# Relation layer of a four-layer graph network: two edge tiles in one expansion product, and keys loaded for two groups at once

## The reference, cut to what matters

```python
rel_in = jnp.concatenate([node_features[src], node_features[tgt]], axis=1)
for r in range(R):                                # R = 4 edge types
    mask = edge_type == r
    rel_t = _lrelu(rel_in @ W_R[r] + b_R[r])      # per edge
    Q = rel_t @ W_Q[r] + b_Q[r]; K = rel_t @ W_K[r] + b_K[r]; V = rel_t @ W_V[r] + b_V[r]
    e = _lrelu(jnp.concatenate([Q, K], axis=1) @ a_w + a_b)[:, 0]
    # softmax of e over the edges of one target and type, then
    h = h + jax.ops.segment_sum(V * attn[:, None], tgt, num_segments=num_nodes)
```

## Time and profile before

| What | Value |
|---|---|
| Time, median of 3 runs | 3078.84 us (3070.05 to 3078.93) |
| Span of the profiled execution | 3100.3 us |
| Own time of the profiled execution | not given apart; its span is 21.5 us over the median |
| PE, PEld busy in the whole span | 2081.7, 1679.2 us |
| DVE, ACT, POOL busy in the whole span | 1578.6, 1176.2, 1685.1 us |
| Group loop of the relation layer | from 107.5 us (first gather) to 800.9 us (last join) |

### The profile page before, as it was taken

How to read it: one execution, slowest core, us unless ns; L and a number is a source line. 1 busy time by engine, 2 the same in 40 slices (tenths; PEclk the granted TensorE clock), 3 DMA queues, 4 the chain that set the end, 5 groups by cost and what they waited for, 6 DMA issues and landing times. The chain is left out here.

```text
span 3100.3 us, 39481 instructions
## 1 busy us (share of the span) xinstructions
PE 2081.7 (67%) x9935; PEld 1679.2 (54%) x9935; DVE 1578.6 (51%) x4421; ACT 1176.2 (38%) x3344; POOL 1685.1 (54%) x1704
## 2 busy tenths in 40 slices
PE   5436777777765778788782356767777656555367
PEld 2235666666654667667671355556655433333267
DVE  4246767676751242423232434657688654444356
ACT  1245556555332223233231344445454322222244
POOL 3366656565104565565643666666646666666600
PEclk9655565656567889889986555555567665565589
DMA  6644444444103223232322444444432222222264
GB/s 223 233 139 128 129 114 136 117 126 115 41 19 86 71 67 80 65 80 65 81 64 73 126 119 120 115 125 123 124 98 70 75 69 78 71 71 72 65 242 141
DMA packets 244614, 322.44 MB, mean 104 GB/s; under 512 B 105346, under 2 KB 160931, under 8 KB 243045
## 3 DMA queue, kind: packets, MB, share of 16 engines
q0 software_dynamic: 66560, 163.90, 18.6%
q1 hardware_dynamic: 177797, 155.67, 16.6%
HBM read 257.60 MB, written 63.38 MB: 104 GB/s over the span
## 5 line engine op out<-in xcount | busy, mean ns | idle before, releaser
L1422 POOL DMA_INDIRECT e_gathered<-msg_src_table,src_idx x416 | 396.6, 953 | 420.9 <-issue 269.2
L703 POOL DMA_INDIRECT e_gathered<-rel_src_table,rel_idx x416 | 433.5, 1042 | 300.3 <-issue 245.6
L1971 POOL DMA_INDIRECT e_kv<-kv_table,src_idx x416 | 410.1, 986 | 275.3 <-issue 195.1
L1985 POOL DMA_INDIRECT rows_by_src<-e_kv,e_row x416 | 419.3, 1008 | 230.2 <-issue 202.0
L2059 PE MATMUL e_ps_q<-e_window,e_spread 64*128 64x128 f32 x1664 | 350.9, 378 | 151.8 <-ACT e_spread L2198 63.6
L2059 PEld LDWEIGHTS e_ps_q<-e_window,e_spread 64*128 64x128 f32 x1664 | 306.9, 275 | 223.8 <-issue 210.9
L2196 ACT ACTIVATE e_spread<-e_offsets,e_minus_lane 64x512 f32<-64x512 f32 x208 | 149.1, 717 | 563.6 <-remote 340.3
L764 PE MATMUL e_ps_r<-e_window,e_spread 64*128 64x128 f32 x832 | 201.0, 413 | 159.3 <-DMA e_window<-rel_dst_table 109.4
L2095 PE MATMUL e_ps_a<-e_onehot,e_weighted 128*128 128x128 f32 (+1 forms) x832 | 185.3, 396 | 144.7 <-issue 67.2
L764 PEld LDWEIGHTS e_ps_r<-e_window,e_spread 64*128 64x128 f32 x832 | 172.3, 304 | 185.5 <-DMA e_window<-rel_dst_table 117.4
L2095 PEld LDWEIGHTS e_ps_a<-e_onehot,e_weighted 128*128 128x128 f32 x832 | 166.5, 297 | 170.9 <-issue 99.3
(11 more groups left out here) (477 smaller groups left out, 4266.0 us busy)
## 6 DMA issues: line engine op xcount, KB each, us to landing
n_rows<-rows_by_src SPq DMA_DIRECT2D x26, 1032.0 KB
e_offsets<-group_offsets SPq DMA_DIRECT2D x208, 128.0 KB
e_keys<-tile_keys SPq DMA_DIRECT2D x104, 128.0 KB
e_window<-rel_dst_table SPq DMA_DIRECT2D x416, 32.0 KB
e_mixed<-in_edge_attr_dram SPq DMA_DIRECT2D x103, 128.0 KB
rel_src_table<-t_up SPq DMA_DIRECT2D x5, 2560.0 KB
e_gathered<-rel_src_table,rel_idx POOLq DMA_INDIRECT x416
e_gathered<-msg_src_table,src_idx POOLq DMA_INDIRECT x416
```

Of the source, the lines that this page charges most:

```text
L703: pool.indirect_dma_start(gathered[:, q % GS, j, :], None, rel_table, bass.IndirectOffsetOnAxis(ap=rel_idx[:, q * J + j:q * J + j + 1], ax ...
L1422: pool.indirect_dma_start(gathered[:, q % GS, j, :], None, msg_table, bass.IndirectOffsetOnAxis(ap=src_idx[:, q * J + j:q * J + j + 1], ax ...
L1971: pool.indirect_dma_start(kv[:, q % RING, j, :], None, kv_table, bass.IndirectOffsetOnAxis(ap=src_idx[:, q * J + j:q * J + j + 1], axis=0) ...
L1985: pool.indirect_dma_start(in_order, bass.IndirectOffsetOnAxis(ap=row[:, q // 2 % RS, q % 2 * J + j:q % 2 * J + j + 1], axis=0), kv[:, slot ...
```

## The change

Two tiles share a product. The stationary operand has 128 partitions: the even tile's keys (j = 0 or 2) on partitions 0 to 63, the odd tile's (j = 1 or 3) on 64 to 127. The moving operand is a block of 128 x 256: the even tile's window rows on partitions 0 to 63 in the first 128 columns, the odd tile's on 64 to 127 in the other 128, and zeros elsewhere. DVE clears the three window buffers once at the layer's start, and SP waits for that before its first load. The output of a product is 128 edges x 256, the first half of the columns for the even tile, the second for the odd one. So the two products of a group replace four.

`keys` and `spread` are 128 partitions x 256 per group in place of 64 x 512. Keys are loaded for two groups at a time, at even q: one transfer for each half of the partitions. `half_lane` is the bias with 64 added on the upper half of the partitions. Gather, join and all that follows are as before.

```diff
-            keys, window = tmp("keys", [NEAR_KEYS, KS, GE]), tmp("window", [NEAR_KEYS, WS, J, D])
-            spread = tmp("spread", [NEAR_KEYS, SS, GE])
+            BATCH, HALF = 2, GE // 2
+            keys, window = tmp("keys", [P, KS, BATCH, HALF]), tmp("window", [P, WS, J, D])
+            spread = tmp("spread", [P, SS, HALF])
+            upper, half_lane = tmp("upper", [P, 1]), tmp("minus_half_lane", [P, P // NEAR])
...
                 def load(q):
                     bases = window_bases([sp.engine], q)
-                    hold(sp, parted_keys, nw * (q - KS + 1))
-                    sp.dma_start(keys[:, q % KS, :], key_row[q:q + 1, :].broadcast_to([NEAR_KEYS, GE])).then_inc(keys_in[q % KS], 16)
+                    if q % BATCH == 0:
+                        b = q // BATCH
+                        hold(sp, parted_keys, nw * BATCH * (b - KS + 1))
+                        for h in range(2):
+                            sp.dma_start(keys[h * NEAR_KEYS:(h + 1) * NEAR_KEYS, b % KS, :, :].rearrange("p g (k e) -> p g k e", e=P),
+                                         key_row[q:q + BATCH, :].rearrange("(a g) (k h e) -> a g k h e", a=1, h=2, e=P)[:, :, :, h, :]
+                                         .broadcast_to([NEAR_KEYS, BATCH, J // 2, P])).then_inc(keys_in[b % KS], 16)
...
                         for j in range(J):
-                            sp.dma_start(window[:, at % WS, j, :], rel_window[bass.ds(bases[j] * R + w * NEAR_KEYS, NEAR_KEYS), :]).then_inc(win_in[at % WS], 16)
+                            half = slice(j % 2 * NEAR_KEYS, (j % 2 + 1) * NEAR_KEYS)
+                            sp.dma_start(window[half, at % WS, j, :], rel_window[bass.ds(bases[j] * R + w * NEAR_KEYS, NEAR_KEYS), :]).then_inc(win_in[at % WS], 16)
...
                 links(0)
+                sp.wait_ge(window_cleared, 1)
...
-                        for j in range(J):
-                            mm = pe.matmul(ps_r[q % 3][:, j, :], spread[:, at % SS, j * P:(j + 1) * P], window[:, at % WS, j, :],
-                                           start=(w == 0 and (nw == 1 or j == 0)), stop=(w == nw - 1), skip_group_check=True)
+                        for k in range(J // 2):
+                            mm = pe.matmul(ps_r[q % 3][:, 2 * k:2 * k + 2, :], spread[:, at % SS, k * P:(k + 1) * P], window[:, at % WS, 2 * k:2 * k + 2, :],
+                                           start=(w == 0 and (nw == 1 or k == 0)), stop=(w == nw - 1), skip_group_check=True)
...
-                    act.wait_ge(keys_in[q % KS], 16 * (q // KS + 1))
+                    act.wait_ge(keys_in[q // BATCH % KS], 16 * 2 * (q // BATCH // KS + 1))
+                    act.wait_ge(halves_told, 2)
...
-                    act.activation(spread[:, at % SS, :], keys[:, q % KS, :], ACT.Abs, bias=key_lane[0:NEAR_KEYS, w:w + 1]).then_inc(parted_keys, 1)
+                    act.activation(spread[:, at % SS, :], keys[:, q // BATCH % KS, q % BATCH, :], ACT.Abs, bias=half_lane[:, w:w + 1]).then_inc(parted_keys, 1)
...
+                dve.memset(window[:, :, :, :], 0.0).then_inc(window_cleared, 1)
+                dve.tensor_scalar(upper[:, :], lane[:, 0:1], float(NEAR_KEYS), float(NEAR_KEYS), ALU.is_ge, ALU.mult).then_inc(halves_told, 1)
+                dve.wait_ge(halves_told, 1)
+                dve.tensor_scalar(half_lane[:, :], key_lane[:, :], upper[:, 0:1], None, ALU.add).then_inc(halves_told, 1)
```

1 line of the change is left out of this document (added).

## The result

The changed kernel takes **3090.69 us** (median of 20 runs, 3073.94 to 3109.07), the kernel before beside it 3080.81 us (20 runs, 3066.97 to 3091.11). The ratio is **1.0037, 95% interval 1.0024 to 1.0050**: slower by 0.37%, some 11 us, a little over what can be told from no change. The forecast was 3078 us and no change.

A forecast was written before the change was run, and what follows sets the result against it. POOL's gathers were taken to pace the relation layer's middle stretch, with at most about 26 us to gain in the loop. Terms 0 - 1 + 0.7 + 0 + 0 gave about -0.3 us, so 3078 us; range 3057 to 3095 us.

The forecast's parts named there:

- no change: Whole kernel: a difference under 0.3%, 9.2 us, which can't be told from none; chance 0.57.
- middle stretch: Relation layer, 243 to 407 us: POOL's gathers set the pace, 6.31 us a group, so an earlier expansion gains nothing.
- first stretch: Relation layer, 110 to 243 us: a shorter expansion chain could gain at most 2.1 us.
- PE, 0: Expansion products: two wide ones stream the same columns as four, 2.07 us at the lower clock; gain 0, bound 0.86 us a group.
- rival B: Expansion on PE: weight loads set its length, so halving them gains 12 to 15 us, 3065 us; chance 0.06.
- ACT, -1 us: Spread on 256 columns saves 0.43 us a group, useful only where PE idles for it: -1 us, bounds 0 to -12.
- rival A: Shorter spread and early keys cut ACT's waits and reach the gathers: 14 us faster, 3065 us; chance 0.17.
- SP, +0.7 us: Two keys transfers delay even groups' windows by 0.66 us; the next odd-group wait absorbs it: +0.7 us, bounds 0 to +16.5.
- rival D: Even groups' windows come too late behind two keys transfers and POOL waits: 16.5 us slower, 3095 us; chance 0.16.
- Pieces of 512 bytes, 0: Keys transfers: 512-byte pieces cost about what 2 KB pieces cost; 0, bounds 0 to +0.3 us a transfer, hidden.
- Clearing on DVE, 0: Start of the layer: clearing the window buffers, 1.3 us, is hidden before SP asks for it; 0.
- rival C: PE's granted clock rises with fuller rows and fewer loads; node stretches give up to 23.7 us, 3055 us; chance 0.04.

The follow-up runs named there:

- e2_four_products: The changed kernel with its two 128x256 products cut into four of 128x128, on a quick chip: 0.9944 of the kernel before.
- e2_changed: The changed kernel itself, unaltered, run again on a quick chip: 0.9939 of the kernel before.
- e4_split: The changed kernel with one of a pair's two keys transfers ahead of each group's windows, on a chip of the slower kind: 1.0049 of the kernel before.
- e1_before_pieces: The kernel before with a group's keys in two transfers of 512-byte pieces in place of one of 2 KB pieces, on a quick chip: 1.0003.
- e4_big_pieces: The changed kernel with keys laid out in DRAM so each keys transfer has 64 pieces of 2 KB, slower kind of chip: 1.0040 of the kernel before.
- e5_rows: The kernel before with its four products over 128 rows, the upper 64 being zero, on a chip of the slower kind: 0.9994.
- the first two groups of experiments: Runs on quick chips: variants of the keys' transfers, then the changed kernel itself and variants; those of the change took 0.9924 to 0.9949 of the kernel before.
- e4_one_transfer: e4_big_pieces with a single keys transfer for a pair of groups in place of two, on a chip of the slower kind: 1.0067 of the kernel before.
- e5_halves: The kernel before with windows on alternate partition halves, keys sent to all 128 partitions, four 128-row products, no pairing; slower kind of chip: 0.9994.

## Why the prediction was wrong

**What bounds the kernel.** For the middle stretch it was right: gathers keep their pace (103 for 104) although PE is busy for 27 us less. For the first stretch it failed, and this is the step that lost the case. I had written that "SP issues the windows just in time in the first stretch", had 66.9 us of waits for windows in the earlier trace rows, and asked only what could be gained there (2.1 us), not what could be lost. I never asked what paced SP. It waits for nobody there; windows come as fast as SP issues them, in bursts of 0.7 us an instruction. I also took the profile's label at its word, 10.7 us of POOL's idle time for expansions: by the 0.75 us between an expansion's end and the gather it was 13.5 us before and is 36.7 us now. The whole loss of this trace, 12 to 13 us, is made there.

**PE, 0: right.** One expansion is again 2.07 us at the lower clock (the row at 184.94 us). Weight loads fell from 172.3 to 103.6 us busy and nothing came of it, so rival B is out, and e2_four_products (8 loads, 0.9944) against e2_changed (4 loads, 0.9939) says so on a quick chip too. The Trainium skill (Perfetto Trace Analysis, Identifying the Most-Contended Engine) names the busy share of LDWEIGHTS, beside the share of peak operations (MFU), as the measure of how close TensorE is to its roofline. I had made a price out of that, which the page doesn't state, and the price didn't come: LDWEIGHTS fell by 69 us in the layer, and the time rose.

**ACT, -1 us: the size of the instructions right, the gain not found.** 500 and 417 ns against about 500 and 416. The waits for keys did not shrink, 112.9 us against 98.7, so rival A is out.

**SP, +0.7 us: the term that failed.** Measured, the last join comes 12.7 us later, near the +16.5 us of the upper bound. "That next wait takes the shift away" is the sentence that failed. SP has no wait in the first stretch that could take a shift up, and POOL's long waits are not for odd groups: they are for groups 4, 8, 12 and 16, 5.7 to 8.4 us each, and they add 23.2 us behind expansions, of which the 15.2 us of POOL's other pauses that they swallow give back only a part. But the mechanism of this term and of rival D, two keys transfers ahead of the even windows, isn't enough as the cause either: e4_split takes it away and has 1.0049. D had the sign, the place (late windows of even groups, PE and POOL idle for them) and about the price, 3095 us for 3090.69. Its reason doesn't hold, so that its price came close is luck. What delays the windows in the changed kernel is not shown.

**Pieces of 512 bytes, 0: right.** e1_before_pieces 1.0003; e4_big_pieces, without them, 1.0040. **Clearing on DVE, 0:** the first gather starts at 106.6 us in place of 107.5; nothing is lost.

**The clock, rival C: its step failed, its price didn't come.** I saw "no reason for it in the rows", and the clock rose from 0.50 to 0.69. e5_rows shows that the 128 rows alone do it. On the chip of the result PE is not the bound where it rose. On quick chips, where gathers are issued at 5.3 us a group from group 1 to 24 and PE is busy for 89% of groups 60 to 84, the higher clock is what these rows offer first for the gain of 0.6%; the 128 rows were not run alone there, nor the shorter spread, so this is argued and not shown.

**The range** of 3057 to 3095 us held 3090.69 us only because D's price was its upper end; "no change" had 0.57 and slower 0.16.

## What to carry to other kernels

When a stretch has many waits for transfers, look next at the queue that issues them: if its engine waits for nobody, its issue is what paces these transfers, and no wait of its own can take up a shift. Check a label of "issue" against the ends of what the program waits for: here it hid 23 of 37 us of one engine's waits for another. Take a change apart on the chip on which it is judged: the same edit was worth -0.6% on one kind and +0.4% on another, and the first two groups of experiments, on the other kind, could say nothing of the loss. And let each cause be undone alone before it is believed: of three plausible stories about the keys' transfers none was enough.

## What the hardware showed that I had not expected

- **Two kinds of chips.** The kernel before takes 2749 to 2752 us on two and 3081 to 3113 us on the others. The relation layer, up to the last join, accounts for 69 us of the 346 us between two traces of the kernel before. The gathers in it last as long on both (1042 and 1059 ns on average). What differs there is POOL's pauses of about 2 us between groups (10 gaps of 1 to 3 us in 88 gathers from 260 to 400 us, and one in 94, with two longer ones at a finished block) and SP's bursts. Where the rest of the 346 us lies was not looked at.
- **SP's bursts.** In them a register instruction with a median of 29 ns takes 0.7 us. They nearly vanish when POOL waits for each group's gathers to land: 3 of some 700 register instructions then take over 0.6 us (110 to 801 us). With four more transfers a group on SP it is 36 of 766 (kernel before) and 52 of 755 (changed), and on another chip of this kind without either edit 110 and 120 of some 830. What makes the bursts is not shown.
- **The granted clock rose with the rows that a product uses.** The kernel before with zeros in the upper 64 rows has a granted clock of 0.66 from 243 to 407 us where 0.50 was granted, with the same count of products and the same results. From 110 to 243 us, where PE is busy for 44 of 133 us, it stays at 0.51, so the rows are not all that counts.
- **One transfer that repeats two sources landed late.** 128 pieces of 2 KB, repeated 64 times from each of two places, have landed 7.9 us after the start of their issue (e4_one_transfer, median up to group 24); 128 pieces of 2 KB repeated from one place after 3.4 us (e5_halves), and two transfers of 64 pieces each after 3.1 us (e4_big_pieces). The DMA packets show why: in e4_one_transfer 1.6 of its packets are under way at a time on average, in e5_halves and e4_big_pieces about 6. The transfer whose source starts with a dimension of 2 was carried by few of the 16 DMA engines.
